# Phase two of a graph kernel with three real products per frequency slot, and 1/rms through memory in phase one

## What is computed

```python
def _L0(x, adj, eps, W1, b1, w, W2, b2):          # H = 512 hidden columns
    agg = eps * x + einsum('bnm,bmd->bnd', adj, x)
    h = agg @ W1 + b1
    h = silu(h * rsqrt(mean(h * h, -1) + 1e-6) * w)
    return h @ W2 + b2
...
# layer 1: 1x1 convolution, batch norm, relu, then a convolution over the nodes
h = relu(bn1(conv1d(xc, conv1_w, 0)))
h = bn2(conv1d(h, conv2_w, 8))                    # 17 taps, 128 x 128 channels
x_conv = relu(h + xc)
# then edge weights, a GRU-like gate, a 3-hop propagation (layer 2), a 2-layer net (layer 3)
```

## Time and profile before

| | |
|---|---|
| time, median of 3 runs | 1124.64 us (1121.78 to 1124.82) |
| profiled execution, its own time | 1127.47 us |
| its span, first to last instruction | 1125.6 us |
| mean granted TensorE clock | 0.984 |
| TensorE busy | 1072.3 us, 95% |
| VectorE, ScalarE, GpSimd busy | 826.1, 715.6, 595.5 us |
| set-up; phase one; phase two; phase three from | 0 to 29.2; 29.2 to 427.8; 427.8 to 490.5; 490.5 us |

### The profile page before, as it was taken

How to read it: one execution, slowest core, us unless ns; L and a number is a source line. 1 busy time by engine, 2 the same in 40 slices (tenths; PEclk the granted TensorE clock), 3 DMA queues, 4 the chain that set the end, 5 groups by cost and what they waited for, 6 DMA issues and landing times.

```text
span 1125.6 us, 24829 instructions
## 1 busy us (share of the span) xinstructions
PE 1072.3 (95%) x8013; PEld 960.3 (85%) x8013; DVE 826.1 (73%) x2548; ACT 715.6 (64%) x1335; POOL 595.5 (53%) x650
## 2 busy tenths in 40 slices
PE   7899999999999969989999999999999999999884
PEld 6799999999999958968888888888888888888774
DVE  4477777777778732634787888888888888889983
ACT  4444555455555522346777878787878787878765
POOL 1244343434334304633576666676767676766674
PEclk9999999999999969999999999999999999999988
DMA  4112332223332125862111111111111111100001
GB/s 163 55 50 85 95 92 87 87 94 95 95 94 79 55 74 163 254 199 65 58 58 48 57 57 58 57 58 58 58 57 58 58 57 58 39 29 11 20 29 38
DMA packets 64190, 84.45 MB, mean 75 GB/s; under 512 B 6464, under 2 KB 33472, under 8 KB 63808
## 3 DMA queue, kind: packets, MB, share of 16 engines
q1 hardware_dynamic: 64064, 82.86, 23.7%
HBM read 57.14 MB, written 25.69 MB: 74 GB/s over the span
## 4 chain that ended last, share of the span: by engine, by line
PE 90%; DVE 3%; issue 2%; ACT 2%; POOL 1%; DMA 1%; SPq 0%; ACTq 0%; DVEq 0%; POOLq 0%
PE banks L160 19%; PE banks L154 11%; PE banks L155 10%; PE banks L156 10%; PE banks L513 10%; PE banks L771 4%; PE banks L541 3%; PE banks L681 3%; PE banks L606 3%; PE banks L656 3%; PE banks L483 2%; PE banks L635 2%; PE banks L721 2%; PE banks L573 1%; PE banks L609 1%
## 5 line engine op out<-in xcount | busy, mean ns | idle before, releaser
L168 POOL TENSOR_TENSOR rstd<-ve,minus_half 128x4 f32<-128x4 f32 x128 | 131.5, 1027 | 72.0 <-DVE ve L1091 66.0
L168 POOL TENSOR_TENSOR r_rms<-ms,minus_half 128x4 f32<-128x4 f32 x32 | 32.3, 1008 | 224.7 <-DVE ms L1055 224.7
L513 PE MATMUL banks<-w,s 128*128 128x128 f32 x768 | 101.2, 275 | 0.4 <-DVE y L1069 0.4
L513 PEld LDWEIGHTS banks<-w,s 128*128 128x128 f32 x768 | 95.6, 192 | 3.4 <-issue 0.5
L154 PE MATMUL banks<-agg_hi,w_hi 128*128 128x512 f32 x192 | 87.5, 455 | 5.7 <-issue 5.5
L1081 DVE BATCH_NORM_STATS2 stats<-y 128x6 f32<-128x128 f32 x384 | 82.9, 279 | 1.7 <-POOL y L1443 1.5
L155 PE MATMUL banks<-agg_lo,w_hi 128*128 128x512 f32 x192 | 77.1, 402 | 0.0
L156 PE MATMUL banks<-agg_hi,w_lo 128*128 128x512 f32 x192 | 76.8, 400 | 0.0
L160 PE MATMUL banks<-at,x_rows 128*128 128x128 f32 x512 | 69.6, 280 | 3.9 <-DVE agg_lo L1043 3.0
L160 PEld LDWEIGHTS banks<-at,x_rows 128*128 128x128 f32 x512 | 65.9, 196 | 7.0 <-issue 2.3
L771 PE MATMUL banks<-w,z 128*128 128x128 f32 x512 | 68.9, 280 | 3.2 <-DVE t L1285 1.9
(11 more groups left out here) (193 smaller groups left out, 3325.4 us busy)
## 6 DMA issues: line engine op xcount, KB each, us to landing
at<-in_at SPq DMA_DIRECT2D x32, 256.0 KB, 2.9
x_rows<-in_x SPq DMA_DIRECT2D x32, 256.0 KB, 2.9
x_scratch<-x SPq DMA_DIRECT2D x32, 256.0 KB, 3.1
ad<-in_ad SPq DMA_DIRECT2D x32, 256.0 KB, 2.6
x1c<-x_scratch SPq DMA_DIRECT2D x32, 256.0 KB, 2.7
atc<-in_at SPq DMA_DIRECT2D x32, 256.0 KB, 2.9
yh<-yh_scratch SPq DMA_DIRECT2D x64, 128.0 KB, 2.8
out<-out_rows SPq DMA_DIRECT2D x32, 256.0 KB, 2.0
```

The lines of the kernel that those rows point to most:

```text
L168: return nc.gpsimd.tensor_tensor(to[:], base[:], minus_half[:], ALU.pow)
L513: last = pe.matmul(bank[7][:, g, :], s[c][:, g, :], w2[:, c, :], start=(c == 0 and g == 0), stop=(c == H0 - 1), skip_group_check=True)
```

## The change

Phase one. `r_rms` is stored to memory (`rms_scratch`, 2 KB a group) and loaded back broadcast to 128 partitions into `rv`, now a ring of two. The four transposes, their bank and ScalarE's copy go. The loaded row is ordered by nodes, then graphs, so the columns of `agg`, `agg_hi`, `agg_lo`, `hn` and `s` are too: `neighbours` writes its PSUM columns four elements apart, and `square_sums` and `down` load their weights four elements (16 bytes) apart. The order of steps on all engines is written anew with other lags, banks are dealt out anew, `agg_hi` and `agg_lo` get two buffers, `AD_RING` goes from 2 to 1, phase one from 43 to 44 turns.

Phase two. Two of three products use differences of the halves, as in three real products for one complex: `shared` = (even - odd of x)(even - odd of w), `own` = even x odd and odd x even with taps' spectrum stored as sum and difference. VectorE and GpSimd make the differences for chunks of four slots (17 chunks), ScalarE halves and copies `shared`, VectorE adds it to `own` for every pair. The staging ring goes from six tiles to four.

```diff
-        X_RING, AT_RING, AD_RING, X1_RING = 4, 2, 2, 2
+        X_RING, AT_RING, AD_RING, X1_RING, RV_RING = 5, 2, 1, 2, 2
+        rms_stored, rv_in = ([sem_of(f"{n}{i}") for i in range(2)] for n in ("rms_stored", "rv_in"))
...
-        STAGES, STORES = 6, 3
+        STAGES, STORES = 4, 3
...
+        def by_node(tile):
+
+            return flat(tile).rearrange("p (n g) -> p g n", g=G)
...
+        CHUNKS = SLOTS // G
+        X_BY_DVE = list(range(0, CHUNKS, 4))
+        X_BY_POOL = [c for c in range(CHUNKS) if c not in X_BY_DVE]
...
-                engine.wait_ge(rest_stored[p], REST_STORES)
+                engine.wait_ge(rest_stored, REST_PAIRS * REST_STORES)
...
+        def difference(engine, out, of, c):
+
+            first = 2 * SLOT_ORDER[G * c]
+            return engine.tensor_tensor(out[c % 2][:], of[:, first:first + 2 * G:2, :],
+                                        of[:, first + 1:first + 2 * G:2, :], ALU.subtract)
...
+            def store_rms(k):
+                until(sp, "r_rms", k)
+                landed(sp, rv_in, k - 2)
+                sp.dma_start(rms_dram[k], r_rms[:]).then_inc(rms_stored[k % 2], 16)
+
+            def load_rv(k):
+                landed(sp, rms_stored, k)
+                until(sp, "hn2", k - RV_RING)
+                sp.dma_start(flat(rv[k % RV_RING]),
+                             rms_dram[k].rearrange("n g -> (n g)").unsqueeze(0).to_broadcast([P, G * P])
+                             ).then_inc(rv_in[k % RV_RING], 16)
...
+                stage(store_rms, t - 1)
+                stage(load_rv, t - 1)
+                stage(load_ad, t + 1 - 12)
                 stage(store_x1, t - 6)
-                stage(load_ad, t + 2 - 11)
...
-            for k in range(2):
-                load_x1(k)
-                load_atc(k)
+            load_x1(0)
+            load_atc(0)
...
+            load_x1(1)
+            load_atc(1)
...
-                by_graph(pe, bank[6], lambda g: x_rows[k % X_RING][:, g, :],
+                by_graph(pe, by_node(bank[4]), lambda g: x_rows[k % X_RING][:, g, :],
...
-            def spread_rms(k):
-                until(pe, "r_rms", k)
-                free(pe, ("hcp", k - 7), ("rv", k - 1))
-                for g in range(G):
-                    last = pe.transpose(bank[4][:, g, :], r_rms[:, g:g + 1].to_broadcast([P, P]), ident[:])
-                last.then_inc(sem["spread"], 1)
...
-                    last = pe.matmul(bank[7][:, g, :], s[c][:, g, :], w2[:, c, :], start=(c == 0 and g == 0),
+                    last = pe.matmul(bank[7][:, g, :], by_node(s[c])[:, g, :], w2[:, c, :], start=(c == 0 and g == 0),
...
                 stage(neighbours, t)
+                stage(down, t - 4, 3)
+                stage(hidden, t - 2, 3)
+                stage(square_sums, t - 1)
+                stage(hidden, t - 2, 2)
                 stage(conv1, t - 8)
+                stage(transform, t - 10, 1)
+                stage(down, t - 3, 0)
+                stage(hidden, t - 1, 1)
+                stage(transform, t - 10, 0)
+                stage(down, t - 3, 1)
+                stage(x1_t, t - 5)
+                stage(hidden, t - 1, 0)
                 stage(down, t - 3, 2)
+                stage(gram, t)
...
+            def shared_products(c):
+                if c in X_BY_DVE:
+                    pe.wait_ge(sem["x_dve"], X_BY_DVE.index(c) + 1)
+                else:
+                    pe.wait_ge(sem["x_pool"], X_BY_POOL.index(c) + 1)
+                pe.wait_ge(sem["w_diff"], c + 1)
+                if c >= 2:
+                    pe.wait_ge(sem["shared"], c - 1)
+                for i in range(G):
+                    if SLOT_ORDER[G * c + i] > 0:
+                        last = pe.matmul(bank[c % 2][:, i, :], x_diff[c % 2][:, i, :], w_diff[c % 2][:, i, :],
+                                         start=True, stop=True)
+                last.then_inc(sem["shared_ps"], 1)
+
+            def own_products(p):
+                if p >= 6:
+                    pe.wait_ge(sem["pair_out"], p - 5)
+                for i in range(2):
+                    slot, psum = SLOT_ORDER[2 * p + i], bank[2 + p % 6]
+                    to_even, to_odd = (2 * slot, 2 * slot + 1) if slot == 0 else (2 * slot + 1, 2 * slot)
+                    pe.matmul(psum[:, 2 * i, :], xh[:, 2 * slot, :], wh[:, to_even, :], start=True, stop=True)
+                    last = pe.matmul(psum[:, 2 * i + 1, :], xh[:, 2 * slot + 1, :], wh[:, to_odd, :],
+                                     start=True, stop=True)
+                last.then_inc(sem["pair_ps"], 1)
 
             until(pe, "xh0", GROUPS - 1)
             until(pe, "xh1", GROUPS - 1)
-            for p in range(PAIRS):
-                if p >= 8:
-                    pe.wait_ge(sem["even_out" if p % 2 == 0 else "odd_out"], (p - 8) // 2 + 1)
-                psum = flat(bank[p % 8])
-                slot_product(psum[:, 0:2 * P], SLOT_ORDER[2 * p])
-                slot_product(psum[:, 2 * P:4 * P], SLOT_ORDER[2 * p + 1]).then_inc(sem["slot_ps"], 1)
+            for c in range(CHUNKS):
+                shared_products(c)
+                own_products(2 * c)
+                own_products(2 * c + 1)
...
+            def shared_out(c):
+                act.wait_ge(sem["shared_ps"], c + 1)
+                if c >= 2:
+                    act.wait_ge(sem["pair_out"], 2 * (c - 1))
+                first = 1 if SLOT_ORDER[G * c] == 0 else 0
+                nc.scalar.activation(shared[c % 2][:, first:G, :], bank[c % 2][:, first:G, :], ACT.Copy, scale=0.5
+                                     ).then_inc(sem["shared"], 1)
...
+                stage(apply0, t - 5)
                 stage(product, t - 1)
+                stage(normalise, t - 3, 2)
+                stage(residual0, t - 4)
                 stage(mean_square, t - 1)
+                stage(normalise, t - 2, 1)
+                stage(stats0, t - 4)
+                stage(low, t)
+                stage(normalise, t - 2, 0)
+                stage(moments, t - 4, 0, LN_EPS)
+                stage(normalise, t - 2, 3)
+                stage(row_sums, t - 12)
                 stage(conv1_bias, t - 8)
...
+            def pair_out(p):
+                dve.wait_ge(sem["pair_ps"], p + 1)
                 stored_pair(dve, p - STAGES)
-                V.tensor_copy(spectrum[p % STAGES][:], bank[p % 8][:]).then_inc(sem["odd_out"], 1)
+                dve.wait_ge(sem["shared"], p // 2 + 1)
+                both, out = bank[2 + p % 6], spectrum[p % STAGES]
+                own = shared[p // 2 % 2][:, 2 * (p % 2):2 * (p % 2) + 2, :]
+                if SLOT_ORDER[2 * p] == 0:
+                    V.tensor_copy(out[:, 0:2, :], both[:, 0:2, :])
+                    V.tensor_tensor(out[:, 2:4, :], both[:, 2:4, :], own[:, 1:2, :].to_broadcast([P, 2, P]),
+                                    ALU.add).then_inc(sem["pair_out"], 1)
+                else:
+                    V.tensor_tensor(out[:].rearrange("p (s h) n -> p s h n", h=2),
+                                    both[:].rearrange("p (s h) n -> p s h n", h=2),
+                                    own.unsqueeze(2).to_broadcast([P, 2, 2, P]), ALU.add).then_inc(sem["pair_out"], 1)
...
+            x_difference(0)
             for p in range(1, PAIRS, 2):
+                pair_out(p - 1)
+                pair_out(p)
+                if p // 2 + 2 in X_BY_DVE:
+                    x_difference(p // 2 + 2)
```

More of the change, by code:

```diff
@@ L198, in graph_layers @@
         last_s, last_hn = rows("last_s"), rows("last_hn")
-        stage_tile = [rows(f"stage{i}") for i in range(3)]
         xh = sb("xh", [P, HALVES, B])
         wh = sb("wh", [P, HALVES, P])
+        rv = [rows(f"rv{i}") for i in range(RV_RING)]
+        x1_rows, agg = rows("x1_rows"), rows("agg")
         y0 = rows("y0")
@@ L238, in graph_layers @@
         row_inv = sb("row_inv", [P, B])
-        x1c = [rows(f"x1c{i}") for i in range(2)]
-        atc = [rows(f"atc{i}") for i in range(2)]
+        x1c, atc = [rows("x1c0")], [rows("atc0")]
         factor, points_lr = sb("factor", [P, 2, P]), sb("points_lr", [P, 2, P])
@@ L583, in _ @@
                 stage(neighbours, t)
+                stage(down, t - 4, 3)
+                stage(hidden, t - 2, 3)
+                stage(square_sums, t - 1)
+                stage(hidden, t - 2, 2)
                 stage(conv1, t - 8)
-                stage(down, t - 3, 2)
-                stage(gram, t - 1)
-                stage(x1_t, t - 5)
-                stage(down, t - 3, 3)
-                stage(transform, t - 10, 0)
-                stage(transform, t - 10, 1)
-                stage(hidden, t - 1, 0)
@@ L884, in rest_high @@
                 copy(rest[:, PART * i:PART * (i + 1), :], rest_full[i % 2]).then_inc(sem["rest_hi"], 1)
-            for p in range(0, PAIRS, 2):
-                slots_out(p)
-                if p >= 14 and (p - 14) // 2 < PARTS:
-                    rest_high((p - 14) // 2)
-                if p == 6:
+            def shared_out(c):
```

(39 more changed lines are left out.)

224 lines of the change are left out of this document (87 added, 137 removed).

## The result

The changed kernel takes 1284.1 us, the median of four runs (1280.6 to 1287.6), against 1124.2 (1121.8 to 1124.8) for the kernel before on the same chip: 1.143 times as long, 95% interval 1.139 to 1.146. The forecast was 1119.6 with a range of 1107 to 1149; the measured time is 164.5 us above the forecast and outside the range.

The account below looks back on a forecast made before the run. TensorE, busy 95% of the span, was taken to bind, with SP's queue almost equally long in phase two. -14.1 + 1.0 - 2.3 + 6.4 + 4.0 = -5.0: 1127.5 to 1122.5 profiled, 1119.6 median; range 1107 to 1149.

Parts of the forecast that it names:

- the term for the strides: Phase one: PSUM writes and weight loads four elements apart cost TensorE zero.
- the upper bound: Phase one: at twice the time per record, `square_sums` and `down` cost 4.5 us a turn, 143 us.
- The rival that named this price: Phase one: strided TensorE accesses are slow, in PSUM and weights, 1291 us; chance 0.05.
- Removed transposes: Phase one: four transposes at 0.44 us a turn go, 32 groups, -14.1 us; period 11.13.
- Fill and drain: Phase one's ends: fill +1.0 us (0 to 4), drain -2.3 (-5 to +1); last `hcp` 15.4 earlier.
- Row sums: End of phase one: one `ad` tile makes each load wait, 11.0 us after the last `hcp`, +6.4 us.
- The row `rv`: Phase one: row back 5.5 us after `r_rms`, 9.5 if slower, with 10 us available; hidden.
- Phase two and the seam: Phase two to phase three: SP and VectorE bind, TensorE's 14.1 us goes into waits; +4 us (0 to +8).
- VectorE's weight work: Start of phase two: the same 4.8 us as before, ahead of the rest loads.
- the first load of the rest: Phase two: `load_rest(0)` comes 29.1 us after the last row sum, 3.7 later than before.
- `load_x1(1)`: Seam to phase three: this load, moved behind, lands in the shadow of the later first `factor`.
- From phase three's first load to the end of the span: Set-up and phase three: phase three's turns are the same, 0 us (-1 to +1).

Follow-up runs that it names:

- The order alone: The kernel before with only the columns ordered by node, then graph (PSUM writes and weight loads four apart), old order of steps: 1271.7 us, ratio 1.132.
- `w` kernels: Changed kernel, TensorE's operands by graph, VectorE reading the row four apart; then earlier row sums; then also fewer rest DMAs: 1134.4, 1127.5, 1120.3 us.
- a_flat_both: The changed kernel with the weights of `down` and `square_sums` both read contiguously (other columns than the result needs): 1121.3 us, ratio 0.998.
- s_stride_2: The kernel before with `down`'s weights read two elements apart (other columns than they should be), one run: 1129.7 us.
- s_stride_3: The kernel before with `down`'s weights read three elements apart (other columns than they should be), one run: 1186.0 us.

## Why the prediction was wrong

**Strides: the step that failed.** It is the term for the strides, put at nothing: "I take zero", from ScalarE's copy out of PSUM. That row shows one engine reading the other memory. For PSUM it led to the right answer, `neighbours` is unchanged, though the row was one of another engine and another direction. For the weights it says nothing, and there the upper bound held: 143 us was worked out, 149 measured for the two alone (120.5 + 28.8). The order alone (1271.7) shows it without anything else of the change. The rival that named this price stood at 1291, with the PSUM stride included, and was given 0.05. The mistake isn't in the arithmetic, it is in the choice: the row taken shared neither the engine, nor the memory, nor the direction with the weight load.

**The clock.** Not foreseen: 13.6 us more when both weights are strided, in turns of 17.3 with the granted clock at about 0.6 for some 4 us. That both together are needed is shown, why the clock falls isn't.

**The rest of the sum** can be read with both weights contiguous (1121.3, 2.5 us under the kernel before; forecast -5.0):
- Removed transposes: turn 11.20 against 11.13. Right in kind, 0.07 a turn less.
- Fill and drain: the first `neighbours` comes at 30.1 instead of 29.2. The last `hcp` ends at 404.9, 19.9 us earlier than before, where 15.4 were forecast. The excess is the clock, not the order: the profiled execution of the kernel before ran its drain at 0.86 in 62.8 us, the same steps took 56.6 at 1.00, and the new order takes 53.4 at 1.00. At equal clock the new order gains 3.2, of which 0.9 are two sets of transposes; the 2.3 left are what was forecast. The prediction took the lower clock of the earlier trace rows for given, and it wasn't.
- Row sums: 12.05 after the last `hcp` instead of 11.0. Right, and the 6.9 that their removal gives in the `w` kernels agrees with the +6.4 (+1) taken.
- The row `rv`: lands 4.1 us after issue, not 2.8, and is hidden, as said.
- Phase two and the seam: phase three's first load is issued 68.1 after the last row sum, 7 later than before. Too small: +4 was taken; from the new phase two alone +7.3 was measured. That SP and VectorE bind and TensorE gains nothing was right up to 625.95. Mis-sized was VectorE's weight work, taken as 4.8 us from the earlier trace rows: from 598.76 to 608.95, without the two copies in between, it is 8.9, and the first load of the rest comes 3.4 later than forecast. Not foreseen was that TensorE then stands in the chain itself, from 625.95 to 642.6, at first at the lower clock. `load_x1(1)`, held to lie in a shadow, stands in the chain of the changed kernel:

```profile
625.95 2.07 PE banks L631 x8
...
645.57 0.62 SPq L420
...
646.90 3.14 DMA x1c<-x_scratch
650.08 1.08 PE banks L665 x16
```

From phase three's first load to the end of the span it is 636.6 us in the changed kernel and 637.6 in `a_flat_both`, against 635.1 before; 0 was taken.

Without the strides the forecast would have been 1.7 us off (2.5 as a difference to the kernel before), and that is in part luck: in the profiled executions the drain's clock gave 6.2 us that nobody had counted, and the seam, the row sums, phase three and the turns took some 8 back.

## What to carry to other kernels

Where a change alters how an operand is laid out, ask for each engine that touches the tile, and each memory, what it does to the element step of that one; the nearest row must share engine, memory and direction, or else the price is unknown and keeps its weight. In these runs a layout turned for the sake of a DMA had a price for all who read it: in memory 4-byte pieces (10.7 us a store), on TensorE double weight loads, on VectorE half again as long; it goes where the reader has slack, or not at all. A stage in which two engines are equally long gains nothing if one of them gets less to do. And a profile is one execution: before a gain is read from a stretch, compare its granted clock with that of the same stretch in another run.

## What the runs showed of the hardware

- float32 weight loads: 1.8 ns per 16-byte line of SBUF when two elements or fewer lie in each; 0.112, 0.1175, 0.175, 0.232 us a record at steps of 1 to 4 (`s_stride_2` and `s_stride_3` are single runs). With one moving column a record takes 0.10, with 128 columns 0.11.
- Writing PSUM four elements apart: no price for records of 0.11 us (8 records 0.89 either way).
- VectorE, one SBUF operand four elements apart: 0.74 to 1.13 us for 128x512.
- VectorE beside GpSimd in phase two: 128x256 0.51 to 1.49 us; 128x128 (`eps_ident`) takes 1.38. GpSimd's difference beside `wt_lo` and `w_lo` takes 2.38 instead of 1.27. That each is the other's reason is argued from their lying side by side; no run takes GpSimd's work away.
- The granted clock fell to 0.6 for 4 us while TensorE was busy without a gap. Its cause is open.
- The same steps at the end of the old phase one, with TensorE idle for part of the time, ran at a granted clock of 0.86, 0.84 and 1.00 in three executions: 62.8, 63.4 and 56.6 us.
